# Two adaLN blocks on one core: the later batches' rows and dense rows kept in DRAM and brought back tile by tile in the first attention group

## The reference

```
h = layernorm(x) * (1 + cb) + sb                  # block 1, second half
dots = softmax(h @ centroids.T / 0.1)
hits = dots > 0.01
query_sel = any(hits, axis=1)                     # per row
row_sel = any(hits, axis=0)[assignments]          # per output column
dense = h @ weight.T + bias
x = x + gb * where(query_sel & row_sel, dense, 0)
...
h = layernorm(x) * (1 + ca) + sa                  # block 2, first half
x = x + ga * attention(h)                         # 32 query heads, 8 key/value heads of 128, causal
```

## Time and profile before

| | us |
|---|---|
| median of 3 runs | 1937.45 (1936.36 to 1938.29) |
| profiled execution | 1937.41 |
| its span | 1935.5 |
| PE busy | 1853.6 (96%) |
| DVE busy | 1242.5 (64%) |
| ACT busy | 1125.4 (58%) |
| POOL busy | 465.2 (24%) |
| DMA | 275.30 MB, mean 142 GB/s |

### The profile page before, as it was taken

One profiled execution on the slowest core, in us unless ns is written; L12 is line 12 of the kernel. 1 busy time (PEld: TensorE's weight loads), 2 busy tenths in 40 slices (PEclk: granted clock), 3 DMA queues, 4 the chain that ended last, 5 costly groups with the idle time before them and its releaser, 6 DMA issues.

```text
span 1935.5 us, 30022 instructions
## 1 busy us (share of the span) xinstructions
PE 1853.6 (96%) x9227; PEld 1546.3 (80%) x9227; DVE 1242.5 (64%) x2974; ACT 1125.4 (58%) x2613; POOL 465.2 (24%) x472
## 2 busy tenths in 40 slices
PE   6887779999999999999999999999999979999999
PEld 3455668888888888888888888888888867888887
DVE  5588766767666666666666666766666676544534
ACT  5564556666666666666666665666666554433423
POOL 3123341423324031222423122240312042010010
PEclk8898889999999999999999999999999999999999
DMA  9101345564656546376654545455453475211010
GB/s 350 71 1 66 122 153 160 158 199 146 188 160 181 166 145 189 112 219 200 185 170 145 178 120 176 146 162 158 144 182 116 145 226 180 66 55 62 9 60 22
DMA packets 170379, 275.30 MB, mean 142 GB/s; under 512 B 18744, under 2 KB 111928, under 8 KB 170304
## 3 DMA queue, kind: packets, MB, share of 16 engines
q1 hardware_dynamic: 169776, 273.32, 45.7%
q10 hardware_dynamic: 528, 1.05, 0.2%
HBM read 173.65 MB, written 100.66 MB: 142 GB/s over the span
## 4 chain that ended last, share of the span: by engine, by line
PE 86%; DVE 5%; ACT 3%; issue 2%; DMA 2%; POOL 1%; SPq 0%; ACTq 0%; DVEq 0%; POOLq 0%
PE ps L1719 25%; PE ps L1791 17%; PE ps L1773 10%; PE ps L1758 9%; PE ps L1922 9%; PE ps L1904 5%; PE ps L1095 1%; PE ps L1777 1%; PE ps L121 1%; PE ps L1755 1%; DVE stats L744 1%; ACT wb L217 1%; PE ps L1025 1%; PE ps L1742 1%; POOL wo L1575 1%
## 5 line engine op out<-in xcount | busy, mean ns | idle before, releaser
L2222 DVE CUSTOM_DVE_ANT_0 ps<-ps,mask 128x512 f32<-128x512 f32 (+3 forms) x512 | 236.4, 524 | 339.6 <-PE ps L1758 339.0
L1719 PE MATMUL ps<-hA,wq 128*128 128x512 f32 x1536 | 387.5, 401 | 4.5 <-DVE qT L2207 4.5
L1791 PE MATMUL ps<-wo,oT 128*128 128x512 f32 x1536 | 373.0, 393 | 8.1 <-POOL wo L1575 5.9
L2045 ACT ACTIVATE pt<-pd 128x1280 fp32r<-128x1280 f32 x128 | 163.1, 1274 | 355.3 <-PE ps L1773 350.4
L1791 PEld LDWEIGHTS ps<-wo,oT 128*128 128x128 f32 x1536 | 287.4, 189 | 67.6 <-POOL wo L1575 6.3
L1719 PEld LDWEIGHTS ps<-hA,wq 128*128 128x128 f32 x1536 | 280.2, 189 | 61.5 <-issue 4.8
L2026 ACT ACTIVATE probs<-ps,nmax 128x512 f32<-128x512 f32 (+3 forms) x512 | 262.7, 532 | 53.6 <-DVE nmax L2222 53.6
L1773 PE MATMUL ps<-pt,V 128*128 128x512 f32 (+2 forms) x1152 | 254.5, 351 | 16.5 <-DVE pt L2246 16.5
L2034 ACT ACTIVATE probs<-probs,rinv 128x512 f32<-128x512 f32 (+3 forms) x512 | 246.2, 552 | 38.9 <-DVE rinv L2228 38.9
L1773 PEld LDWEIGHTS ps<-pt,V 128*128 128x128 f32 x1152 | 198.2, 191 | 43.7 <-issue 18.9
L1758 PE MATMUL ps<-kT,qT 128*128 128x512 f32 (+2 forms) x1152 | 225.1, 340 | 0.0
(11 more groups left out here) (231 smaller groups left out, 2634.6 us busy)
## 6 DMA issues: line engine op xcount, KB each, us to landing
turned_blocks<-tp SPq DMA_DIRECT2D x128, 640.0 KB, 3.0
pd<-turned_blocks SPq DMA_DIRECT2D x512, 160.0 KB, 3.3
wq_next<-in_L_attn_w_q_dram SPq DMA_DIRECT2D x16, 1024.0 KB, 5.8
wo_in<-in_L_attn_w_o_dram SPq DMA_DIRECT2D x16, 1024.0 KB, 6.7
wm<-in_L_wmod_dram SPq DMA_DIRECT2D x6, 2048.0 KB, 13.5
X<-in_L_attn_x_dram SPq DMA_DIRECT2D x4, 1024.0 KB, 11.4
wk_in<-in_L_attn_w_k_dram SPq DMA_DIRECT2D x16, 256.0 KB, 3.9
wv_in<-in_L_attn_w_v_dram SPq DMA_DIRECT2D x16, 256.0 KB, 4.2
```

Of the source, the lines that this page charges most:

```text
L1719: last = nc.tensor.matmul(ps[:, bank, :], w[i][:, c, cols], hT[k][:, c, b * S:(b + 1) * S], start=(c == 0 and n == 0), stop=(c == DC - 1 a ...
L1791: last = nc.tensor.matmul(ps[:, bank, :], oT[x_][:, b, h, r * P:(r + 1) * P], wo[y_][:, h, :], start=(h == 0 and n == 0), stop=(h == GQ - ...
L2045: nc.scalar.activation(flat(pt[0][:]), flat(pd[:, u % 2]), ACT.Copy).then_inc(phi_done, 1)
L2222: nc.vector.tensor_tensor_reduce(out=v, in0=v, in1=mask[:, TB * P - KEYS[i]:], scale=-1.0, scalar=3e38, op0=ALU.add, op1=ALU.min, accum_ou ...
```

## The change

The rows and dense rows of batches 2 and 3 are written to a new DRAM tensor `later_rows`, in four DMAs of 1 MB: the rows when the attention of block 1 has been added, the dense rows of batch 2 and batch 3 when they are drained. SP waits for all four (`rows_kept`) before group 0. Two slots of two tiles each (`later_slots`: rows and dense rows) take their place on chip. In group 0 SP fetches tiles 0 and 1 in unit 0, 2 and 3 in unit 1, 4 and 5 in unit 2, 6 in unit 3, 7 in unit 4 (`FETCHED`); DVE works on tiles 0 and 1 in unit 1, 2 and 3 in unit 2, then one per unit (`LATER`); a slot is fetched into again after its store to `x_mid` has landed. The gate rows of batches 2 and 3 are multiplied by the hit columns once (`hit_gates`), so that a tile is finished by one gating, one addition and the moments, without a select. The output weights are loaded in unit 2 of group 0 as in the other groups. Three smaller moves: `linear(14)` goes behind the cluster choice, the second inverse of batch 0 ahead of the selects of batch 1, and the square root of the later batches from ACT's unit 5 to 6 (its reciprocal from DVE's unit 6 to 7). Two load semaphores are merged.

```diff
@@ first_sync
+                sp.wait_ge(x1_done, NT)
+                for i in range(PAIR):
+                    sp.dma_start(later_rows[0, i], X[PAIR + i][:]).then_inc(rows_kept, 16)
+                sp.wait_ge(drained, NT - TB)
+                sp.dma_start(later_rows[1, 0], dense[PAIR][:]).then_inc(rows_kept, 16)
                 for t in range(PAIR * TB):
-                    store_row(sp, t)
...
+                    sp.wait_ge(x2_done, t + 1)
+                    sp.dma_start(mid_t[t // TB][:, t % TB, :], rows(X, t)).then_inc(mid_stored, 16)
+                sp.wait_ge(drained, NT)
+                sp.dma_start(later_rows[1, 1], dense[PAIR + 1][:]).then_inc(rows_kept, 16)
+                sp.wait_ge(rows_kept, 64)
...
+            LATER = {1: (0, 1), 2: (2, 3), 3: (4,), 4: (5,), 5: (6,), 6: (7,)}
+            FETCHED = {0: (0, 1), 1: (2, 3), 2: (4, 5), 3: (6,), 4: (7,)}
+
+            def fetch_tile(sp, n):
+                for k in range(2):
+                    sp.dma_start(later_slots[n % 2][k][:], later_rows[k, n // TB, :, n % TB, :]).then_inc(ld_x[n % 2], 16)
...
+            def hit_gates(dve):
+
+                dve.wait_ge(chosen, COLS_COPIED)
+                for b in range(PAIR, B):
+                    last = nc.vector.tensor_tensor(gb_rows[:, b, :], gb_rows[:, b, :], hit_cols[:], ALU.mult)
+                link_vector(dve, last)
+
+            def later_tile(dve, n):
+                t = PAIR * TB + n
+                x_, d_ = later_slots[n % 2]
+                dve.wait_ge(ld_x[n % 2], 16 + 32 * (n // 2 + 1))
+                link_vector(dve, nc.vector.scalar_tensor_tensor(d_[:], d_[:], qsel[:, t:t + 1], gb_rows[:, t // TB, :],
+                                                                ALU.mult, ALU.mult))
+                link_vector(dve, nc.vector.tensor_tensor(x_[:], x_[:], d_[:], ALU.add))
+                nc.vector.bn_stats(stats[:, t, :], x_[:]).then_inc(x2_done, 1)
@@ first_tensor
                 linear(13)
-                linear(14)
                 pe.wait_ge(chosen, TOP_FOUND)
...
+                linear(14)
                 linear(15)
@@ sync, body
-                                if at_group(g, 0) and u < TB:
-                                    store_row(sp, PAIR * TB + 2 * u)
-                                    store_row(sp, PAIR * TB + 2 * u + 1)
-                                if at_group(g, 0) and u == 4:
-
-                                    sp.wait_ge(mid_stored, 16 * NT)
+                                if at_group(g, 0):
+                                    if u == 0:
+
+                                        sp.wait_ge(low_2, DC // 2 + DC)
+                                    for n in LATER.get(u, ()):
+                                        store_tile(sp, n)
+                                    if 1 <= u <= 6:
+                                        sp.wait_ge(mid_stored, 16 * (PAIR * TB + LATER[u][-1] + 1))
+                                    for n in FETCHED.get(u, ()):
+                                        fetch_tile(sp, n)
...
-                                if u == (4 if at_group(g, 0) else 2):
+                                if u == 2:
                                     load_out(g)
@@ vector, body
-                                if first and u <= TB:
-                                    later_gated(u)
+                                if first and u in LATER:
+                                    later_tile(dve, LATER[u][0])
...
-                                if first and u < TB:
-                                    later_selected(u)
+                                if first and u == 0:
+                                    hit_gates(dve)
+                                if first and len(LATER.get(u, ())) > 1:
+                                    later_tile(dve, LATER[u][1])
```

More of the change, by code:

```diff
@@ L136, in adaln_two_blocks @@
         with ExitStack() as early:
-            sb(early, "kept_xr", [P, TB, P], F32)
-            hit_cols = sb(early, "hit_cols", [P, D], F32)
+            later_slots = [[sb(early, f"later{k}", [P, D], F32) for k in range(2)]]
         wb = sb(ctx, "wb", [P, WB, D], BF16)
@@ L228, in adaln_two_blocks @@
         with l0:
+            later_rows = nc.dram_tensor("later_rows", [2, PAIR, P, TB, D], F32, kind="Internal").ap()
+            rows_kept = sem("rows_kept")
             with ExitStack() as early:
@@ L283, in adaln_two_blocks @@
                 cen_in = sb(early, "cen_in", [NCL, D], F32)
+            with ExitStack() as early:
+                hit_cols = sb(early, "hit_cols", [P, D], F32)
             dense[0] = sb(l0, "dense0", [P, TB, D], F32)
@@ L322, in adaln_two_blocks @@
             NSLOT = 3
-            ld_c, ld_w, ld_b, ld_cw, ld_ffn = (sem(n) for n in ("ld_c", "ld_w", "ld_b", "ld_cw", "ld_ffn"))
+            ld_c, ld_w, ld_b, ld_ffn = (sem(n) for n in ("ld_c", "ld_w", "ld_b", "ld_ffn"))
             ld_wm = [sem(f"ld_wm{k}") for k in range(len(MODS) // 2)]
@@ L401, in first_sync @@
                 load_x(2)
-                sp.dma_start(cen_in[:], cent).then_inc(ld_cw, 16)
-                sp.dma_start(w_in[:], ffn_w.rearrange("(c p) i -> p c i", p=P)).then_inc(ld_cw, 16)
+                sp.dma_start(cen_in[:], cent).then_inc(ld_ffn, 16)
+                sp.dma_start(w_in[:], ffn_w.rearrange("(c p) i -> p c i", p=P)).then_inc(ld_ffn, 16)
                 sp.dma_start(bias_r[:], ffn_b.rearrange("(o d) -> o d", o=1).to_broadcast([P, D])).then_inc(ld_ffn, 16)
@@ L1119, in first_tensor @@
                 turn_mod(3)
-                pe.wait_ge(ld_cw, 32)
+                pe.wait_ge(ld_ffn, 64)
                 for c in range(DC):
@@ L1307, in adaln_two_blocks @@
                     gate_r = sb(early, "gate_r", [P, PAIR, D], F32)
+                with ExitStack() as early:
+                    later_slots.append([sb(early, f"later{k}", [P, D], F32) for k in range(2)])
                 hp = [sb(at, f"hp{i}", [P, S], F32R) for i in range(2)]
@@ L2103, in body @@
                                     p_high(g, u - 1)
-                                if first and u == 5:
+                                if first and u == 6:
                                     act.wait_ge(var_2, 4)
@@ L2270, in prologue @@
                             dve.wait_ge(consts, CONSTS + 2)
-                        def later_tiles(u):
-                            return range(PAIR * TB + 2 * u, PAIR * TB + 2 * u + 2)
-                        def later_gated(u):
-                            if u < TB:
-                                for t in later_tiles(u):
-                                    last = gate_row(dve, t)
-                                link(last)
-                            if 1 <= u <= TB:
-                                for t in later_tiles(u - 1):
-                                    last = moments(t)
-                                if u == TB:
-                                    link(last)
-                                    variances_2(dve, range(PAIR * TB, NT), var_2)
-                        def later_selected(u):
-                            if u == 0:
-                                dve.wait_ge(chosen, COLS_COPIED)
-                            for t in later_tiles(u):
-                                last = add_row(t)
-                            link(last)
-                            for t in later_tiles(u):
-                                select_row(t, hit_cols[:])
-                            dve.wait_ge(x2_done, later_tiles(u)[-1] + 1)
                         def body(g, turns):
@@ L2309, in body @@
                                     chunk_low(g, u // 4)
-                                if first and u <= TB:
-                                    later_gated(u)
+                                if first and u in LATER:
+                                    later_tile(dve, LATER[u][0])
                                 if first and u == 6:
+                                    dve.wait_ge(x2_done, NT)
+                                    variances_2(dve, range(PAIR * TB, NT), var_2)
+                                if first and u == 7:
                                     dve.wait_ge(std_late, 1)
```

19 lines of the change are left out of this document (10 added, 9 removed).

## The result

| | before | after |
|---|---|---|
| median of 5 runs, us | 1938.29 (1936.36 to 1942.56) | 1958.31 (1952.65 to 1962.33) |
| profiled execution, us | 1937.41 | 1957.57 |
| ratio | | 1.0096, 95% interval 1.0073 to 1.0119 |

The change makes the kernel slower by 1.0%. The forecast was 1952.8 us in 1940 to 1963, slower with 88%. The profiled executions are 20.2 us apart, and that is the number that the rows have to explain.

What follows compares the result with a forecast made beforehand. PE never idles from about 290 us, so earlier delay is carried to the end; -1.9 + 4.55 + 12.1 + 5.8 + 1.4 - 1.0 - 5.6 = +15.4 us on 1937.4 gives 1952.8 us, range 1940 to 1963.

Steps and rivals of the forecast that it cites:

- a closed round: Group 0, units 1 to 3: write, read, store, fetch and tile wait on one another; DVE stalls 26.8 us in sum.
- T6: Moment SP starts writing unit 6's turned probabilities (T0 to T5 likewise for units 0 to 5); 20.95 us late.
- Start: Start of layer 2 up to unit 0's write: linear tile 14 and second inverse moved, less gating; -1.9 us.
- Unit 1: DVE stands still until tile 0 is fetched, 10.8 us after unit 0's write; +4.55 us.
- Units 2 and 3: Stores must land before the next fetch, in unit 2 behind the 1 MB query weights; +12.1 and +5.8 us.
- Unit 4: Tile 5 comes along with tile 4, no wait; its 2.05 us replace two moments and the variances; 0.
- Unit 5: One tile of 2.05 us in a place where DVE idled 0.6; +1.4 us.
- Unit 6: Tile 7 and the variances run beside ACT's exponentials, two table loads moved to unit 7; -1.0 us.
- Output weights: Load moves from unit 4 to unit 2, so unit 7's scores no longer wait for the split; -5.6 us.
- The hidden fetches: Rival, units 1 to 3: every tile is there when DVE asks, kernel faster; -11.4 us, 1926 us; 5%.
- the rival of the collisions: Rival, group 0: fetches and the output-weight load run into the bounce; +9.5 us, 1962 us and beyond; 5%.
- the sum by its fit for each DMA alone: Group 0 landings at about 2.0 us plus bytes at 436 GB/s; total +4.9 us instead of +15.4.

Runs made afterwards that it cites:

- a lighter queue: The change with the 1 MB query-weight load in unit 1 of group 0 issued behind the stores and fetches: 1953.74 us, ratio 1.0063.
- the fetch in the bounce: The opened round with the fetch issued between the write of the turned probabilities and the wait for its landing: 1917.61 us, ratio 0.9880.
- the opened round: The change with one tile at a time, fetched a unit or more ahead, done behind the turning, query weights last: 1921.85 us, ratio 0.9920.

## Why the prediction came out as it did

The mechanism was right: a closed round whose waits fall in units 1, 2 and 3 and end when tile 5 is fetched along with tile 4. DVE's waits were 6.89, 13.89 and 8.00 us against 6.4, 13.2 and 7.2, PE idled 16.9 us in unit 2 (over 10 was named), unit 4 had no wait, T1, T2 and T3 were 231.5, 255.6 and 274.1 against 229, 253 and 271. The experiments bear it out on three sides: an earlier fetch takes away the wait of unit 1 and leaves most of the others, a lighter queue shortens unit 2 and leaves units 1 and 3, and the traffic without the round costs the whole nothing measurable. Of the 4.8 us that are missing (20.2 against 15.4), 4.1 stand in T6, which is 25.1 late against 20.95:

- *Start, forecast -1.9, measured -0.3.* The edit gave what I worked out, or more (2.4 us from the cluster choice to T0), but this execution reached it 2.1 us later than the one of before. I set one execution against another and had no term for their scatter, which the eight traces of the new order put at 4.9 us.
- *Unit 1, +4.55 against +5.5.* The tile was there at T0 + 11.2 instead of 10.8, and its gating took 1.27 us instead of 0.70, beside POOL's split of the keys' weights (below).
- *Units 2 and 3, +12.1 and +5.8 against +12.6 and +6.1.* The stores took what the loaded rows said (9.4 us from the first store's issue to the fetch). From the fetch's issue to the gating it took 4.1 and 4.0 us, where I had 3.35.
- *Unit 4, 0 against -0.5.*
- *Unit 5, +1.4 against +4.05.* The step that failed. I put the tile's 2.05 us in the place of 0.6 us of idle time and took the 7.64 before for the unit's own length. The tile took 2.92 us, in the place of 0.58, which makes +2.34, and the low part of the probabilities behind it +0.3. Both ran beside POOL's splits; with the load put back to unit 4, which moves the splits away, the tile takes 2.11 us and unit 5 10.64 instead of 11.69, so the overlap costs 1.05. The other 1.4 I had no term for: before, PE's scores of unit 5 started 0.31 us after T4, at 264.91, and took 1.75, after the change 1.00 us after T4, at 288.24, and 2.61:

```profile
265.22 1.75 PE L1758 MATMUL ps<-kT,qT 128*128 128x512 f32 x9
```

```profile
289.24 2.61 PE L1804 MATMUL ps<-kT,qT 128*128 128x512 f32 x9
```

- *Unit 6, -1.0 against -2.3.* 12.92 was no length of its own either: there the scores came 1.77 us after T5, here 0.33. With a tile ahead of the reciprocal PE waits 0.8 to 1.3 us for DVE in units 5 to 7, and the pace is 10.62; before, PE ran through unit 5 without a wait. So only the two units together, +1.75 against +0.4, show what the tiles cost there.
- *Output weights, -5.6 against -5.7.* Right, though not what the early load is worth in the changed kernel: without it, about 12 us.

The hidden fetches, given 5%, did not come in this order of the queue. Their time, 1926 us, lies 4 to 8 us above what versions with few or no waits for tiles gave, 1921.9 and 1917.6. One slip in the rival of the collisions: the 5.1 us of a bounce write are in the trace (237.86 to the read-back at 243.00) but not in the earlier trace rows.

On the rule of the page "DMA: Bandwidth & Descriptors" of the Trainium skill (section "Anatomy of one DMA"): the sum by its fit for each DMA alone, +4.9, is refuted by +20.2. That fit is for DMAs of the GpSimd path, and these are SP's. The same fit, taken over all bytes that SP had issued just ahead, which the page doesn't state, does better. For the two stores behind the 1 MB load it gives 2.0 us and 1.5 MB at 436 GB/s, an estimate of 5.6 us, and 7.1 with the four read-backs of 160 KB; the row shows a median of 7.8. Without the load ahead the same two sums give 3.2 and 4.7, and the row shows 3.8.

## What to carry to other kernels

When a buffer goes through store, landing, fetch and use, count the landings that follow one another in one turn of it, and compare them with the time of a unit: from T1 to tile 2's use they were 2.9, 9.4 and 4.1 us, in a unit that had 11.6. With the same transfers fetched a unit ahead, and the tile's work behind the turning instead of ahead of the reciprocal, 8.5 us of waits were left of 28.8, and none with the fetch in the bounce. The two moves were made together, and what each is worth was not measured. On a queue that is served in order, put a wait where the queue would stand still anyway, behind the issue that others need and ahead of a landing that it must await, and put the large load behind what the next step needs. Take the pace of a unit from the steady stretch, not from one row that may be catching up, and measure terms from the nearest common event, not from the start of the span.

## What the runs showed beyond that

- Two 256 KB stores of one unit land after 3.8 us or after 7.8 (median of the two), by whether 1 MB was issued just ahead of it. The 640 KB bounce write took about 3 us elsewhere; in the opened round, with a fetch, a store and 1 MB ahead, its read-back was issued 7.5 us after it (228.40 to 235.87).
- The start of this kernel scatters by 4.9 us between executions, loosely along with where PE's clock is at its lower level; the runs of one version differ by 6 to 14 us.
- DVE's gating takes 0.73 to 0.75 us as a rule, but up to 1.8 where it meets an instruction of POOL, and POOL gets longer too. In the change, DVE's tile 5 and POOL at the same time:

```profile
293.47 1.26 DVE L776 SCALAR_TENSOR_TENSOR later<-later,qsel,gb_rows 128x512 f32<-128x512 f32 x1
294.76 0.98 DVE L778 TENSOR_TENSOR later<-later,later 128x512 f32<-128x512 f32 x1
```

```profile
292.88 1.30 POOL L1622 TENSOR_TENSOR wo<-wo_in,wo 128x512 fp32r<-128x512 f32 x1
294.12 1.07 POOL L1613 CAST wq<-wq_next 128x512 fp32r<-128x512 f32 x1
295.28 1.62 POOL L1615 TENSOR_TENSOR wq<-wq_next,wq 128x512 fp32r<-128x512 f32 x1
```

The addition takes 0.98 instead of 0.69, POOL's cast 1.07 instead of 0.61 and its subtraction 1.62 instead of 1.30. The 1.27 us of tile 0 have the same neighbour, POOL's split at 225.51 to 226.77.

Left open: what sets the place of the lower clock in the first 60 us, and whether two tiles per unit, or a tile still ahead of the reciprocal, would also do if they were fetched a unit ahead; that was not tried.
